# Queries and keys as three bf16 parts through a DRAM scratch into three buffers, bf16 masks and row maxima, and a new order of all engines

## The chip, the cores and the metric

The kernel runs on one core of one Trainium2 chip. The metric is the device time of one execution in microseconds, lower is better. A core has TensorE (PE in the profile; its weight loads are PEld), VectorE (DVE), ScalarE (ACT), GpSimd (POOL) and SyncE (SP), which run their own queues in order and meet at semaphores.

## The reference, cut to what matters

Two transformer layers over x of shape (16, 256, 128), 16 heads of width 8, each layer attention and then a mixture of experts, with a layer norm behind each of the four parts:

```python
x = layernorm(x + attn0(x))      # causal, no biases
x = layernorm(x + moe0(x))       # 8 experts, top 2, hidden 256, relu
x = layernorm(x + attn1(x))      # not causal, biases
x = layernorm(x + moe1(x))       # 15 experts, top 3, gelu gate, and a shared expert
# attention, for each batch b and head h (T = 256, 8 columns per head):
s = q @ k.T / sqrt(8)            # causal in layer 0
p = softmax(s); o = p @ v
```

All inputs and outputs are fp32.

## The kernel before

The work is cut into steps; a step is one batch, or one batch and one head, or one page of an expert. The 32 attention steps a = 0 to 31 are the 16 batches of layer 0 and then of layer 1. A planner (`plan` and `lay_out`) gives every step a cost, a due time from the table `PRM` and its predecessors, simulates the five engines, and so writes the one order in which every engine issues its steps. The order is fixed when the kernel is built; on the chip every engine runs its own part of it strictly in order, held back by semaphores alone.

For a batch, TensorE makes q and k with one projection (`qk`, bank M). Every fp32 matmul of the program stands in the trace as two (128 records of L1056 for 64 matmuls), and q and k are not multiplied in fp32: they are split into a rounded high part (`qk_hi`, ScalarE, type fp32r) and the rest (`qk_lo`, VectorE, fp32r), both in the tile `parts`. SyncE then stacks them with DMAs (`stack(a, u)`, half u = 8 heads) from `parts` straight into one of four buffers `QK`, 24 rows per head: hi with hi, hi with lo, lo with hi. One fp32r matmul over the stacked rows then gives nearly fp32 scores. Each head's scores are computed twice: `scores` with queries on partitions, from which VectorE takes row maxima (`row_max`), and `scores_T` with keys on partitions, which ScalarE exponentiates. Between them, the negated maxima are split in two fp32r parts (`max_neg`), transposed (`max_T`), copied (`max_keep`) and put by a DMA from ScalarE's queue (`max_rows`) into rows 96 and 97 of the same `QK` buffer, against rows of ones, so that `scores_T` comes out with the maximum already subtracted. In layer 0 a first matmul writes the causal mask (identity times a mask, both fp32r in `rmat`) into the diagonal blocks of each bank. A `QK` buffer of half a batch is refilled when `scores_T` of the half two batches earlier is done.

`weigh_V` multiplies the exponentials by V (fp32), `O_T`, `O_back` and `proj` finish the attention, and `x_T2`, `logits`, `ranks` route the tokens. When 8 (layer 1: 10, then 6) batches are routed, VectorE builds the group's table, GpSimd scatters the rows of X to expert order in DRAM with indirect DMAs (`scatter`, L877), and the pages of 256 tokens go through their expert (`page_T`, `fc1`, `fc2`). GpSimd gathers the results back (`gather`, L891), VectorE combines them, and the next layer's batch can start. GpSimd also computes the inverse standard deviations of all norms, in the same queue. There are 23, 23, 44 and 32 pages in the four groups.

```python
def free(k):                                  # PE waits here for a bank
def stack(a, u):                              # SP: parts -> QK[2a+u mod 4], three DMAs
    sp.wait_ge(st_ps.sem, st_ps.at(a - 2, 8 * u + 8))
```

Of the kernel before, what the change touches and what calls it, by code (L numbers as in the profile page):

```python
# [6 lines left out]
F32R = mybir.dt.float32r  # L7
# [21 lines left out]
PAGE = 256  # L29

# [120 lines left out]
def shared_y_bank(b):  # L151
# [17 lines left out]
       "shift": (-30.67, 4.18, -7.9, 46.33, 16.49, 43.17, -9.93, -50.66, -60.0, 2.38, -45.61, -29.2, 39.76, 32.2, -40.19, 42.55, -0.37, -36.42, 17.74, 2.5, -8.66, -6.21, 7.29, 60.0, -16.96, -0.13, -5.19, 52.25, -27.76, -60.0, -17.49, -25.48),  # L169
       "ld": (131.0, 350.8, 247.85, 156.55, 400.0), "clear": (312.1, 268.62), "comb": 330.3}  # L170


def plan():
# [18 lines left out]
    def attention(a, t):  # L192
# [3 lines left out]
        S = (0.35, 0.245)[L]  # L196
# [7 lines left out]
        add(t + qk[0], "PE", 0.87, 0.25, "qk", a, after=x + [("stack", a - 1, 0), ("stack", a - 1, 1)], bank="M")  # L204
        add(t + qk[1], "ACT", (0.64, 0.95)[L], 0.1, "qk_hi", a, after=[("qk", a)])
        add(t + qk[2], "DVE", (0.72, 0.9)[L], 0.1, "qk_lo", a, after=[("qk_hi", a)], frees="M")
        add(t + PRM["v"][ph], "PE", 0.44, 0.25, "v", a, after=x + [("weigh_V", a - 3, 3)], bank="M")
        add(t + PRM["v"][ph] + 0.6, "ACT", 0.4, 0.1, "v_keep", a, after=[("v", a)], frees="M")
        t += PRM["first"][ph]
        for u in range(2):  # L210
            heads = range(8 * u, 8 * u + 8)
            add(t, "SP", 2.03, PRM["l_stack"] if a else 7.0, "stack", a, u, after=[("qk_lo", a)] + [("scores_T", a - 2, h) for h in heads])
            t += PRM["lag_s"][ph]
            for h in heads:
                add(t, "PE", S, 0.25, "scores", a, h, after=[("stack", a, u), ("max_neg", a - 2, u)], bank=("S0", "S1")[h % 2])
# [3 lines left out]
            add(t + mx[0], "DVE", (0.68, 0.6)[L], 0.1, "max_neg", a, u, after=[("row_max", a, h) for h in heads] + [("max_T", a - 1, u)])  # L219
# [42 lines left out]
    def chunk(c, t, step):  # L262
# [70 lines left out]
    for i in range(len(X_PIECES)):  # L333
        add(PRM["ld"][0] + PRM["ld"][1] * i, "SP", 0.95 if i == 0 else 0.5, 6.0, "load_x", i, after=[("stack", max(1, 2 * i), 1)])
    add(PRM["ld"][2], "SP", 3.3, 3.0, "load_later", after=[("stack", 3, 0)])
    add(PRM["ld"][3], "DVE", 3.0, 0.1, "prepare", after=[("load_later",), ("stack", 4, 1)])
    add(PRM["ld"][3] + 60, "PE", 0.3, 0.25, "bias_rows", after=[("prepare",), ("stack", 6, 1)], bank="N")
    add(PRM["ld"][3] + 60, "DVE", 0.4, 0.1, "bias_add", after=[("bias_rows",)], frees="N")
    for k, (lo, hi) in enumerate(TAB_PIECES):
        add(PRM["ld"][4] * 0.25 + P[0] * k, "SP", 1.2 * (hi - lo), 6.0, "build_w1", k, after=[("prepare",), ("stack", 5 + k, 1)])  # L340
    for k in range(len(FILL_STEPS)):
        add(PRM["clear"][0] + PRM["clear"][1] * k, "SP", 0.5, 3.5, "clear_xs", k, after=[("stack", 1 + k // 2, k % 2)])
# [99 lines left out]
def build(nc, x_in, xT_in, cols_in, rows_in, bmat_in, rmat_in, wqk_in, wvo_in, w0_in, w1_in, w2_in, b2_in, sw1_in, out):  # L442
    ctx = ExitStack()
    with ctx:
# [13 lines left out]
        parts = sb("parts", [D, 2, 2, T], F32R)  # L458
        QK = [sb(f"QK{i}", [D, NH // 2, 2, T], F32R) for i in range(4)]
# [1156 lines left out]
```

## Time and profile before

| | |
|---|---|
| median of 3 runs | 1208.55 us (1205.19 to 1209.41) |
| span of the profiled execution, first to last instruction | 1058.9 us |
| outside the span (median less span) | 149.65 us |
| busy in the span | PE 906.3, PEld 763.1, DVE 679.9, ACT 549.4, POOL 444.0 us |
| mean granted TensorE clock | 0.927 |

The profile does not give the profiled execution a time of its own beyond its span, so what lies around the span is taken as the median less the span. Busy time of PE counts modelled ends of pipelined matmuls, so a stretch in which PE is "busy" throughout is one in which it never ran dry, not one at its peak.

### The profile page before, as it was taken

To read this page: it belongs to the slowest core of one execution; us is meant where nothing else is said; L and a number is where in the kernel's file an instruction comes from. 1 tells how busy PE (TensorE), PEld (TensorE's weight loads), DVE (VectorE), ACT (ScalarE), POOL (GpSimd) and SP (SyncE) were. 2 spreads that over 40 slices of the span, in tenths; PEclk is the share of its full clock that TensorE was granted. 3 is DMA by queue.
4 is the path that set the end of the run, shared out by engine and by line. 5 is a ranking of instruction groups with operands and counts; after the bars stand their busy time and mean duration, and the time that the engine had idled before them with its cause. 6 is when DMAs were issued, how large, how long until landed. Compare 5 with 4: busy or idle time off the path is not lost.

```text
span 1058.9 us, 23206 instructions
## 1 busy us (share of the span) xinstructions
PE 906.3 (86%) x7486; PEld 763.1 (72%) x7486; DVE 679.9 (64%) x2209; ACT 549.4 (52%) x1320; POOL 444.0 (42%) x688
## 2 busy tenths in 40 slices
PE   5899988995999996998999896899898999789910
PEld 4788878884899985766888665676666789688810
DVE  3467755673644475987655566888875565378863
ACT  1356654562655564666766474567556655334300
POOL 7000100054500075477200375325776157377774
PEclk9699998997999998999999897999989999989965
DMA  4557564555468433364667333323444789888421
GB/s 78 103 107 193 114 142 101 135 135 133 106 178 204 125 68 59 53 125 85 144 182 191 66 57 58 51 35 56 87 90 130 216 264 326 280 247 270 122 64 53
DMA packets 111752, 138.49 MB, mean 131 GB/s; under 512 B 12275, under 2 KB 86033, under 8 KB 111633
## 3 DMA queue, kind: packets, MB, share of 16 engines
q1 hardware_dynamic: 100241, 114.97, 45.9%
q0 software_dynamic: 10240, 20.99, 7.9%
q10 hardware_dynamic: 1152, 1.05, 0.6%
q8 instruction: 62, 1.02, 0.4%
q14 instruction: 57, 0.47, 0.2%
HBM read 70.25 MB, written 42.48 MB: 106 GB/s over the span
## 4 chain that ended last, share of the span: by engine, by line
PE 49%; DMA 20%; issue 8%; POOL 7%; DVE 7%; SPq 6%; ACT 2%; POOLq 0%; ACTq 0%; DVEq 0%
DMA QK<-parts 10%; PE bank_O L1132 5%; PE bank_N L1224 5%; DMA G<-yd,ypos 5%; PE bank_FH L1212 4%; POOL xs L877 4%; PE bank_S L1087 4%; PE bank_T L1110 3%; PE bank_S L1083 3%; PE bank_S L1085 3%; PE bank_T L1114 3%; SPq L736 2%; PE bank_T L1112 2%; PE bank_M L1056 2%; DMA QK<-mrow 2%
## 5 line engine op out<-in xcount | busy, mean ns | idle before, releaser
L1298 DVE TENSOR_REDUCE mp<-bank_S 128x3 f32<-128x384 f32 (+1 forms) x512 | 304.2, 620 | 133.9 <-PE bank_S L1087 91.7
L948 ACT ACTIVATE P<-bank_T 128x384 f32<-128x384 f32 (+1 forms) x512 | 260.9, 543 | 90.0 <-PE bank_T L1114 58.2
L891 POOL DMA_INDIRECT G<-yd,ypos x160 | 155.2, 970 | 76.1 <-issue 47.3
L877 POOL DMA_INDIRECT xs<-X,ypos x160 | 155.9, 974 | 48.7 <-issue 43.6
L1132 PE MATMUL bank_O<-P,V 128*32 128x256 f32 (+1 forms) x2048 | 128.8, 371 | 1.4 <-ACT P L948 1.0
L1083 PE MATMUL bank_S<-QK 96*128 96x256 f32 x512 | 112.4, 322 | 18.5 <-DMA QK<-parts 8.9
L1110 PE MATMUL bank_T<-QK 128*128 128x256 f32 x512 | 110.8, 322 | 10.6 <-ACT P L948 6.1
L828 POOL TENSOR_TENSOR rstd<-mv,half 128x2 f32<-128x2 f32 x48 | 9.6, 200 | 261.4 <-DVE mv L1351 261.1
L1085 PE MATMUL bank_S<-rmat 128*128 128x256 f32 x256 | 91.7, 358 | 22.3 <-DMA QK<-parts 21.6
L1083 PEld LDWEIGHTS bank_S<-QK 96*128 96x128 f32 x512 | 79.5, 201 | 35.8 <-DVE mp L1298 20.5
L1087 PE MATMUL bank_S<-QK 96*128 96x128 f32 (+1 forms) x512 | 104.7, 292 | 0.0
L1110 PEld LDWEIGHTS bank_T<-QK 128*128 128x128 f32 x512 | 78.7, 201 | 30.5 <-ACT P L948 20.6
L1112 PE MATMUL bank_T<-rmat 128*128 128x256 f32 x256 | 87.3, 341 | 2.4 <-DMA QK<-mrow 2.4
L1114 PE MATMUL bank_T<-QK 128*128 128x256 f32 (+1 forms) x512 | 88.7, 255 | 0.0
L955 ACT ACTIVATE OT<-bank_O 128x256 f32<-128x256 f32 x128 | 48.8, 382 | 74.1 <-PE bank_O L1132 72.8
L1132 PEld LDWEIGHTS bank_O<-P,V 128*32 128x32 f32 x2048 | 55.1, 112 | 43.1 <-issue 9.6
L1087 PEld LDWEIGHTS bank_S<-QK 96*128 96x128 f32 x512 | 85.6, 204 | 0.4
L1517 DVE SCALAR_TENSOR_TENSOR X<-G,wk,X 128x128 f32<-128x128 f32 x160 | 55.5, 351 | 45.7 <-DMA G<-yd,ypos 41.5
L1114 PEld LDWEIGHTS bank_T<-QK 128*128 128x128 f32 x512 | 81.0, 194 | 0.3
L1085 PEld LDWEIGHTS bank_S<-rmat 128*128 128x128 f32 x256 | 51.6, 202 | 33.2 <-issue 25.1
L842 POOL TENSOR_TENSOR dm<-lg,m 128x16 f32<-128x16 f32 (+1 forms) x32 | 7.5, 234 | 123.2 <-DVE m L1382 122.8
L1000 ACT ACTIVATE hT<-bank_FH,W 128x256 f32<-128x256 f32 x92 | 38.6, 470 | 39.6 <-PE bank_FH L1212 38.9
(171 smaller groups left out, 1753.3 us busy)
## 6 DMA issues: line engine op xcount, KB each, us to landing
QK<-parts SPq DMA_DIRECT2D x192, 128.0 KB
QK<-wtab SPq DMA_DIRECT2D x76, 257.0 KB, 3.9
W<-w_in SPq DMA_DIRECT2D x46, 321.0 KB, 4.0
QK<-xs SPq DMA_DIRECT2D x38, 256.0 KB, 4.3
yd<-P SPq DMA_DIRECT2D x38, 256.0 KB, 3.9
xs<-zeros SPq DMA_DIRECT2D x17, 512.0 KB, 8.1
xp<-xs SPq DMA_DIRECT2D x22, 256.0 KB, 4.1
yd<-yb SPq DMA_DIRECT2D x22, 256.0 KB, 4.0
```

The lines of the kernel that those rows point to most:

```text
L877: pool.indirect_dma_start(xs[g % 2], bass.IndirectOffsetOnAxis(ypos[L][:, 2 * b + blk, k:k + 1], 0), X[:, 2 * b + blk, :], None).then_inc( ...
L891: pool.indirect_dma_start(G[i][:, blk, k, :], None, yd[g], bass.IndirectOffsetOnAxis(ypos[L][:, 2 * b + blk, k:k + 1], 0))\
L948: act.activation(P[:, (h // 4) % 2, h % 4, 0:n], bank[("T0", "T1")[h % 2]][:, 0:n], ACT.Exp, scale=SCALE)\
L1083: m = pe.matmul(S[:, qb * T:(qb + 1) * T], Q[:, qb * D:(qb + 1) * D], K)
L1085: pe.matmul(diagonal(S), identr, mask_q, start=True, stop=False, skip_group_check=True)
L1087: m = pe.matmul(S[:, o:o + n], Q[:, qb * D:(qb + 1) * D], K[:, 0:n], start=False, stop=(qb == 1), skip_group_check=True)
L1110: m = pe.matmul(S[:, kb * T:(kb + 1) * T], K[:, kb * D:(kb + 1) * D], Q)
L1112: pe.matmul(diagonal(S), identr, mask_k, start=True, stop=False, skip_group_check=True)
L1114: m = pe.matmul(S[:, o:o + n], K[:, kb * D:(kb + 1) * D], Q[:, kb * D:T], start=False, stop=(kb == 1), skip_group_check=True)
L1132: m = pe.matmul(o, w, x, start=(kb == 0), stop=(kb == 1), skip_group_check=True)
L1298: dve.tensor_reduce(mp[:, a % 2, 0:n, h], bank[("S0", "S1")[h % 2]][:, 0:n * w] .rearrange("p (a c) -> p a c", a=n), AX.X, ALU.max).then_i ...
L1517: dve.scalar_tensor_tensor(out=t, in0=G[i][:, blk, k, :], scalar=wk[L][:, b, blk, k:k + 1], in1=t, op0=ALU.mult, op1=ALU.add).then_inc(sig ...
```

## The change

Queries and keys are split in three bf16 parts, hi, mid and low. ScalarE makes hi (`qk_hi`), VectorE the fp32 rest (`qk_rest`), ScalarE mid (`qk_mid`, new) and VectorE low (`qk_low`, new). SyncE writes the six slots to a DRAM scratch (`spread_parts`, new, two scratches by turns), and from there fills 48 rows of one whole batch buffer (`stack(a)`): hi·hi, hi·mid, mid·hi and further pairs. There are three buffers of a whole batch instead of four of half a batch; a buffer is refilled after `scores_T` of the batch three earlier. The row maxima come out of the reduction already negated and are split in three bf16 pieces by reading the upper halves of fp32 words; their transpose is a bf16 matmul and they take three rows. The mask matmul is bf16 and the fp32r table `rmat` is gone. The planner's costs and its table of due times are new, so the order of every engine changes.

```diff
-        parts = sb("parts", [D, 2, 2, T], F32R)
-        QK = [sb(f"QK{i}", [D, NH // 2, 2, T], F32R) for i in range(4)]
+        parts = sb("parts", [D, 2, 3, T], BF16)
+        rest = sb("rest", [D, 2, T])
+        QK = [sb(f"QK{i}", [D, 2, NH, T], BF16) for i in range(3)]
...
-            def stack(a, u):
-                c = 2 * a + u
+            def spread_parts(a):
                 sp.wait_ge(lo_done.sem, lo_done.all(a))
-                if a < 2:
-                    sp.wait_ge(cleared.sem, 1 + 3 * c)
-                    if c == 0:
+                if a >= 2:
+                    sp.wait_ge(stacked[(a - 2) % 3].sem, stacked[0].all((a - 2) // 3))
+                sp.dma_start(stk[a % 2].rearrange("i p t -> p i t"), slots(parts[:, :, :, :])).then_inc(spread[a % 2].sem, DMA)
+
+            def stack(a):
+                sp.wait_ge(spread[a % 2].sem, spread[a % 2].all(a // 2))
+                if a < 3:
+                    sp.wait_ge(cleared.sem, 1 + 3 * a)
+                    if a == 0:
                         sp.wait_ge(cleared_dve.sem, 2)
                 else:
-                    sp.wait_ge(st_ps.sem, st_ps.at(a - 2, 8 * u + 8))
-                p = parts[64 * u:64 * u + 64, :, :, :].bitcast(F32).rearrange("p s i t -> p (s i) t")
-                for i, pair in enumerate((p[:, 0::2, :], p[:, 0::3, :], p[:, 1:3, :])):
-                    sp.dma_start(QK[c % 4][HD * i:HD * i + HD, :, :, :].bitcast(F32), pair).then_inc(stacked[c % 4].sem, DMA)
+                    sp.wait_ge(st_ps.sem, st_ps.all(a - 3))
+                for row, n in ((0, 3), (3, 2), (5, 1)):
+                    pair = stk[a % 2].rearrange("i (d h) t -> (i d) (h t)", h=NH).rearrange("(s r) c -> r s c", s=2) if n == 3 else \
...
+                    sp.dma_start(QK[a % 3][row * HD:(row + n) * HD, :, :, :].rearrange("r s h t -> r s (h t)"), pair)\
+                        .then_inc(stacked[a % 3].sem, DMA)
...
+            def qk_mid(a):
+                act.wait_ge(rest_done.sem, rest_done.all(a))
+                act.activation(slots(parts[:, :, :, :])[:, 1::3, :], rest[:, :, :], ACT.Copy).then_inc(mid_done.sem, 1)
...
-                if h % 8 == 0:
-                    pe.wait_ge(stacked[c % 4].sem, stacked[c % 4].all(c // 4))
+                if h == 0:
+                    pe.wait_ge(stacked[a % 3].sem, stacked[a % 3].all(a // 3))
...
-                    pe.matmul(diagonal(S), identr, mask_q, start=True, stop=False, skip_group_check=True)
+                    pe.matmul(diagonal(S), identb, mask_q, start=True, stop=False, skip_group_check=True)
...
+            def qk_low(a):
+                dve.wait_ge(mid_done.sem, mid_done.all(a))
+                p = slots(parts[:, :, :, :])
+                dve.tensor_tensor(p[:, 2:4, :], rest[:, :, :], p[:, 1::3, :], ALU.subtract).then_inc(lo_done.sem, 1)
...
-       "period": (49.67, 34.69, 165.68), "first": (30.17, 13.12, 29.81, 163.03),
+       "period": (50.52, 67.62, 161.84), "first": (0.0, 36.41, 64.77, 143.39), "lag_s": (51.57, 41.8, 6.21, 26.18),
```

Two places show what the new table does. The first is TensorE at the seam of the layers: the rows just ahead of the first head of layer 1, batch 16 (`bank_S0<-QK`, L1083 before and L1099 after). `bank_T` rows are heads of `scores_T`, here of batch 15, `bank_O` is `weigh_V`. Before:

```order
L1112 MATMUL bank_T1<-rmat 128x2x128
L1114 MATMUL bank_T1<-QK2 128x256
L1114 MATMUL bank_T1<-QK2 128x128
L1140 MATMUL bank_N<-cols,OT 128x128 x4
L1096 MATMUL bank_M<-cols,neg 16x128 x2
L1112 MATMUL bank_T0<-rmat 128x2x128
L1114 MATMUL bank_T0<-QK2 128x256
L1114 MATMUL bank_T0<-QK2 128x128
L1112 MATMUL bank_T1<-rmat 128x2x128
L1114 MATMUL bank_T1<-QK2 128x256
L1114 MATMUL bank_T1<-QK2 128x128
L1083 MATMUL bank_S0<-QK0 128x256 x2
```

And with the change:

```order
L1154 MATMUL bank_N<-cols,OT 128x128 x4
L1201 MATMUL bank_N<-mk0,bmat 128x8
L1202 MATMUL bank_N<-mk0,bmat 128x8
L1203 MATMUL bank_N<-mk0,bmat 128x8
L1204 MATMUL bank_N<-mk0,bmat 128x8
L1205 MATMUL bank_N<-mk0,bmat 128x8
L1060 MATMUL bank_M<-cols,X 128x128 x2
L1154 MATMUL bank_N<-cols,OT 128x128 x4
L1085 MATMUL bank_M<-wvo,xT 128x128 x2
L1162 MATMUL bank_N<-cols,On 128x128 x2
L1099 MATMUL bank_S0<-QK1 128x256 x2
```

Before, most heads of `scores_T` of batch 15 still stood behind the first head of batch 16; now batch 15 is finished up to its output transposes (`O_T`, L1154) when batch 16 begins.

The second place is SyncE's queue in layer 0, around the refill for batch 6 (`xs` is the DRAM buffer being cleared, `wtab` a table of weights being built, `xT` the transposed input of a batch to come). Before:

```order
L715 DMA xs1<-zeros 512x1x256
L720 DMA wtab<-w1_in 256x258
L722 DMA wtab<-xG1 128x2x128
L723 DMA wtab<-b2 256x1x128
L715 DMA xs1<-zeros 512x1x256
L692 DMA xT<-xT_in 128x256
L736 DMA QK0<-parts 8x16x256 x2
L736 DMA QK0<-parts 8x8x512
L736 DMA QK1<-parts 8x16x256 x2
L736 DMA QK1<-parts 8x8x512
```

And with the change:

```order
L731 DMA wtab<-w1_in 256x258
L733 DMA wtab<-xG1 128x2x128
L734 DMA wtab<-b2 256x1x128
L726 DMA xs1<-zeros 512x1x256
L703 DMA xT<-xT_in 128x256
L726 DMA xs1<-zeros 512x1x256
L754 DMA QK0<-stk0 24x2x4096
L754 DMA QK0<-stk0 16x2x4096
L754 DMA QK0<-stk0 8x2x4096
L740 DMA stk1<-parts 128x6x256
```

The same neighbours stand ahead of the refill, which is now three DMAs for the whole batch instead of six, with the parts of the next batch sent to the scratch right behind it.

## Rows read from the trace of the kernel before

**Rows 1.** Stretches: length, busy (instructions) of PE, PEld, DVE, ACT, POOL, clock, DMA.

```profile
60.00:140.00 80.00, 78.97 (x798) 69.51 (x797) 57.84 (x194) 48.60 (x119) 7.53 (x28) 1.00 0.65 140
18.00:219.50 201.50, 188.16 (x1757) 165.57 (x1756) 131.91 (x419) 103.06 (x252) 17.97 (x57) 0.93 0.58 122
219.50:290.00 70.50, 55.72 (x547) 48.98 (x546) 41.41 (x153) 33.18 (x82) 38.70 (x59) 0.90 0.55 132
290.00:370.00 80.00, 80.00 (x675) 73.31 (x674) 35.14 (x108) 45.25 (x119) 2.51 (x10) 1.00 0.68 167
370.00:406.00 36.00, 34.88 (x362) 30.18 (x361) 27.94 (x108) 24.89 (x64) 27.36 (x46) 1.00 0.45 75
406.00:450.00 44.00, 34.75 (x293) 27.52 (x293) 33.68 (x108) 22.02 (x55) 19.94 (x37) 0.88 0.31 49
450.00:512.00 62.00, 55.00 (x473) 42.02 (x472) 48.81 (x162) 41.57 (x93) 43.99 (x69) 0.94 0.53 108
512.00:592.00 80.00, 78.04 (x616) 68.47 (x615) 41.89 (x108) 50.37 (x126) 5.06 (x14) 1.00 0.69 166
592.00:643.00 51.00, 38.61 (x337) 27.34 (x337) 30.02 (x114) 28.14 (x65) 30.27 (x49) 0.85 0.34 59
643.00:722.00 79.00, 70.36 (x564) 55.02 (x562) 66.17 (x219) 48.52 (x115) 29.44 (x66) 0.90 0.31 45
722.00:829.00 107.00, 96.35 (x831) 69.98 (x830) 75.21 (x251) 69.27 (x157) 72.89 (x106) 0.95 0.47 106
829.00:1058.90 229.90, 168.84 (x1040) 150.61 (x1039) 143.45 (x464) 79.74 (x192) 139.08 (x155) 0.88 0.67 203
```

**Rows 2.** Waits of PE from 18 to 290 us: total, times, longest.

```profile
PE bank_S L1085 <- DMA QK<-parts: 21.4, 7, 12.4
```

**Rows 3.** PE in order of time: start, length, engine, line (layer 0).

```profile
101.00 0.38 PE L1112 MATMUL bank_T<-rmat 128*128 128x256 f32 x1
...
101.81 0.38 PE L1148 MATMUL bank_N<-cols,On 128*128 128x128 f32 x2
```

**Rows 4.** Groups of 60 to 140 us: times | busy us, mean ns | idle.

```profile
L1085 PE MATMUL bank_S<-rmat 128*128 128x256 f32 x64 | 22.0, 344 | 0.7 <-DMA QK<-parts 0.7
```

**Rows 5.** The chain that ended last, 190 to 205 us: start, us, one head.

```profile
202.80 0.12 PE bank_S L1085
202.92 0.23 PE bank_S L1087 x2
```

**Rows 6.** PE in order of time: bf16 matmuls and their loads.

```profile
662.08 0.17 PE L1188 MATMUL bank_N<-mk,bmat 128*128 128x15 bf16 x1
...
662.16 0.17 PE L1191 MATMUL bank_N<-mk,bmat 128*128 128x15 bf16 x1
```

**Rows 7.** Groups of the whole span: the splits and layer 1's row maxima.

```profile
L1298 DVE TENSOR_REDUCE mp<-bank_S 128x2 f32<-128x512 f32 x256 | 167.5, 686 | 36.6 <-PE bank_S L1083 35.5
...
L1285 DVE TENSOR_TENSOR parts<-bank_M,parts 128x512 fp32r<-128x512 f32 x16 | 11.0, 686 | 5.6 <-ACT parts L912 5.6
L912 ACT ACTIVATE parts<-bank_M 128x512 fp32r<-128x512 f32 x16 | 9.5, 596 | 14.8 <-PE bank_M L1056 14.8
```

**Rows 8.** The chain that ended last, whole span: start, us, what.

```profile
138.92 6.15 SPq L696
...
150.82 10.57 DMA QK<-parts
...
195.86 6.22 DMA QK<-parts
```

**Rows 9.** DMA issues of the whole span: count, KB each, median us to landing.

```profile
QK<-wtab SPq DMA_DIRECT2D x76, 257.0 KB, 3.9
```

**Rows 10.** GpSimd's scatters of 450 to 512 us: ns min/median/max, first and last start.

```profile
L877 POOL DMA_INDIRECT xs<-X,ypos x32: 954/959/1082, 457.2 to 503.6; - x32
```

**Rows 11.** The same of 722 to 829 us.

```profile
L877 POOL DMA_INDIRECT xs<-X,ypos x60: 954/958/1103, 729.6 to 816.0; - x60
```

**Rows 12.** GpSimd's gathers of 829 us to the end, the same columns.

```profile
L891 POOL DMA_INDIRECT G<-yd,ypos x96: 940/944/1029, 918.9 to 1044.2; - x96
```

More of the change, by code:

```diff
@@ L203, in attention @@
         x = [("load_xT", a), ("load_consts",)] if L == 0 else [("x_T_keep", a), ("load_later",)]
-        add(t + qk[0], "PE", 0.87, 0.25, "qk", a, after=x + [("stack", a - 1, 0), ("stack", a - 1, 1)], bank="M")
+        add(t + qk[0], "PE", 0.87, 0.25, "qk", a, after=x + [("spread_parts", a - 1)], bank="M")
         add(t + qk[1], "ACT", (0.64, 0.95)[L], 0.1, "qk_hi", a, after=[("qk", a)])
-        add(t + qk[2], "DVE", (0.72, 0.9)[L], 0.1, "qk_lo", a, after=[("qk_hi", a)], frees="M")
+        add(t + qk[2], "DVE", (0.72, 0.9)[L], 0.1, "qk_rest", a, after=[("qk_hi", a), ("qk_low", a - 1)], frees="M")
+        add(t + qk[2], "ACT", 0.63, 0.1, "qk_mid", a, after=[("qk_rest", a)])
+        add(t + qk[2], "DVE", 0.63, 0.1, "qk_low", a, after=[("qk_mid", a)])
+        add(t + qk[2], "SP", 0.68, 3.4, "spread_parts", a, after=[("qk_low", a), ("stack", a - 2)])
         add(t + PRM["v"][ph], "PE", 0.44, 0.25, "v", a, after=x + [("weigh_V", a - 3, 3)], bank="M")
@@ L209, in attention @@
         t += PRM["first"][ph]
+        add(t, "SP", 2.03, 4.6, "stack", a, after=[("spread_parts", a), ("scores_T", a - 3, 15)])
         for u in range(2):
             heads = range(8 * u, 8 * u + 8)
-            add(t, "SP", 2.03, PRM["l_stack"] if a else 7.0, "stack", a, u, after=[("qk_lo", a)] + [("scores_T", a - 2, h) for h in heads])
             t += PRM["lag_s"][ph]
             for h in heads:
-                add(t, "PE", S, 0.25, "scores", a, h, after=[("stack", a, u), ("max_neg", a - 2, u)], bank=("S0", "S1")[h % 2])
+                add(t, "PE", S, 0.25, "scores", a, h, after=[("stack", a), ("max_T", a - 2, u)], bank=("S0", "S1")[h % 2])
                 add(t + 0.4, "DVE", (0.58, 0.71)[L], 0.1, "row_max", a, h, after=[("scores", a, h)],
@@ L218, in attention @@
                 t += PRM["step_s"][ph]
-            add(t + mx[0], "DVE", (0.68, 0.6)[L], 0.1, "max_neg", a, u, after=[("row_max", a, h) for h in heads] + [("max_T", a - 1, u)])
+            add(t + mx[0], "DVE", (0.68, 0.6)[L], 0.1, "max_neg", a, u, after=[("row_max", a, h) for h in heads])
             add(t + mx[1], "PE", 0.25, 0.25, "max_T", a, u, after=[("max_neg", a, u), ("max_rows", a - 1, u)], bank="M")
@@ L439, in all, with build @@
         return (i + 1) * self.per
[L442 removed]
+def build(nc, x_in, xT_in, cols_in, rows_in, bmat_in, wqk_in, wvo_in, w0_in, w1_in, w2_in, b2_in, sw1_in, out):
     ctx = ExitStack()
@@ L542, in build @@
         wtab = dram("wtab", (E1, D, WCOLS[1]))
+        stk = [dram(f"stk{i}", (SLOTS, D, T), BF16) for i in range(2)]
         bank = {n: ctx.enter_context(nc.psum_tensor(f"bank_{n}", [D, 2 * T], F32)) for n in BANKS}
@@ L580, in build @@
         v_kept = signal("v_kept")
-        stacked = [signal(f"stacked{i}", 3 * DMA) for i in range(4)]
+        spread = [signal(f"spread{i}", DMA) for i in range(2)]
+        stacked = [signal(f"stacked{i}", 3 * DMA) for i in range(3)]
         s_ps = signal("s_ps", NH)
@@ L588, in build @@
         m_kept = signal("m_kept", 2)
-        m_stacked = [signal(f"m_stacked{i}", DMA) for i in range(4)]
+        m_stacked = [[signal(f"m_stacked{i}{u}", DMA) for u in range(2)] for i in range(3)]
         st_ps = signal("st_ps", NH)
@@ L1057, in qk @@
                 m.then_inc(qk_ps.sem, 1)
-                held["M"] = lo_done.sem, lo_done.all(a)
+                held["M"] = rest_done.sem, rest_done.all(a)
             def v(a):
@@ L1590 @@
     mask_q = np.where(after, f32(NEG), f32(0))
-    bmat = np.concatenate([after.astype(f32), np.ones((D, D), f32)], axis=1).astype(ml_dtypes.bfloat16)
-    rmat = np.stack([np.eye(D, dtype=f32), mask_q, mask_q.transpose(1, 0)], axis=1)
+    bmat = np.concatenate([after.astype(f32), np.ones((D, D), f32), np.eye(D, dtype=f32), mask_q, mask_q.transpose(1, 0)],
+                          axis=1).astype(ml_dtypes.bfloat16)
     arrays = {
```

155 lines of the change are left out of this document (75 added, 80 removed), and 14 rows, old and new, of the table PRM.

## The prediction

> **What bounds the kernel now.** I read the profile by stretches first, cut where one thing hands over to the next: 18 us is the first head of `scores`, 219.5 the routing of batch 7 (`ranks`), 290 and 370 the first and last page of group 0, 406 the first head of layer 1, 450 the routing of batch 15, 512 and 592 the pages of group 1, 643 the first head of batch 24, 722 the routing of batch 25, 829 the first page of layer 1 [rows 1]. In layer 0's attention TensorE is never dry: 79.0 of the 80 us from 60 to 140 are busy at full clock, while VectorE has 57.8 and ScalarE 48.6 [rows 1]. 64 heads of `scores` stand in that stretch, four batches, so 20.0 us a batch [rows 4]. The waits come second: from 18 to 290 us PE waited 21.4 us for refills of `QK` (7 times, longest 12.4 us) and for hardly anything else [rows 2]. The chain says why: `x_in`'s issue held SyncE 6.2 us before a refill that took 10.6 us itself, and even an undisturbed one, at 195.9 us, takes 6.2 us [rows 8].
>
> Two further bounds are not TensorE's. Between a group's routing and its first page GpSimd must scatter: 32 scatters from 457.2 to 503.6 us sit between 450 and 512 [rows 1, 10], 60 from 729.6 to 816.0 between 722 and 829 [rows 1, 11]. And the end is GpSimd's as well: 96 gathers, one each 1.32 us, from 918.9 to 1044.2 us [rows 12]. In layer 1's attention no engine is full: 70.4 of 79 us PE, 66.2 DVE [rows 1], 0.686 us per head for the row maximum alone [rows 7].
>
> **A head in bf16.** A `scores` and a `scores_T` head of layer 0 together take 101.81 - 101.00 = 0.81 us, 0.405 each [rows 3]; in the chain's best case one takes 0.12 + 0.23 = 0.35 [rows 5]. That is three weight loads and 256 + 128 + 256 columns. In bf16 the columns stay. 256 of them took 0.12 us with the fp32r load beside them, so 640 take at most 0.30 us [rows 5]. Loads: four starts from L1188 to L1191, each with a full bf16 load ahead of it, are 0.08 us apart, 27 ns each [rows 6], so a bf16 load hides under any of the three matmuls. I take 0.29 us (bounds: 0.27, which is 640 columns at one per cycle of the 2.4 GHz level that the rows grant, and 0.35, the best fp32r head). It saves 0.115 us a head, 32 heads a batch: 3.7 us of 20.0.
>
> The Trainium skill speaks against this. "TensorE: Matmul & The Clock Gate", section "LDWEIGHTS (loading the stationary operand)", gives a load of P columns P/1.2 ns whatever the type, 107 ns for 128; an estimate from it is 3 x 107 = 320 ns a head, and the head saving would shrink by a quarter or more. Its section "Weight-path perf modes" lets non-fp32 loads of 128 columns go faster. By the first the trace disagrees (27 ns for load and matmul together), by the second it agrees.
>
> The shorter transposes of the maxima are worth about 0.1 us each, 0.2 a batch. In layer 1 a head has two matmuls of 256 columns at 0.12 us or so; at 0.107 to 0.12 the gain is 0 to 0.4 us a batch, and VectorE's 0.686 us paces those heads anyway. I count none.
>
> So TensorE needs 16.2 us per batch of layer 0. VectorE has 57.84 / 4 = 14.5 now, and `qk_low` comes to it: between nothing and 0.686, the price of the same shape from PSUM [rows 7]; I take 0.6, which makes 15.1. ScalarE has 48.6 / 4 = 12.2 and gets `qk_mid`, 0.6 [rows 7]. `max_neg` keeps its number of operations. Three engines at 16.2, 15.1 and 12.8 don't mesh perfectly: I take 17.3 us a batch.
>
> **Refills.** Before, each half batch took three DMAs and its landing 6.2 to 10.6 us [rows 8]. Now `parts` goes to DRAM and back. The trip out has no row; I take 2 to 8 us around it, and it stands beside work: `qk` of a batch now stands 23 to 28 us of TensorE work ahead of its first head in batches 3 to 10, where it was 9 to 11. What can be late is `stack(a)`, which waits for the last `scores_T` of batch a-3. Counted in the new order with the durations above, TensorE has 9.1, 5.2, 6.0, 6.7, 6.9, 7.9, 9.8, 9.0, 12.8, 11.9, 10.2, 17.8, 6.9 us of work between that and the first head, for a = 3 to 15, and 4.8 to 8.5 for five batches of layer 1 (19 and 22 to 25); elsewhere over 11. The landing of 768 KB in three DMAs is bounded by 3.9 us, that of 257 KB in long runs [rows 9], and 10.6 [rows 8]; its runs are 8 KB against 1 KB, so I take 7, and a shortfall of under 2 us for five batches, 5 us in all. Behind `stack(a)` on SyncE wait the next `spread_parts`, `xT`, the clearing of `xs` and `wtab`'s pieces, all due later than the head. The longest stalls (12.4 us) came with SyncE held by loads ahead of a refill needed at once; `qk` early and whole batches ahead remove that, in part.
>
> **The new order.** All steps keep their predecessors; what changes is which stand together. Stretch by stretch, before and after:
> - start to first head: 18, after 21 (`spread_parts` 2 to 4 us, two more splits 1.2, against two fewer fp32r tables).
> - to batch 7 routed: 201.5. Ten batches less 2.7 us each, less 8 of the stalls of this stretch, plus 11 more heads of `scores` now placed here (3) and 5 for late refills: 173.
> - to the first page: 70.5. TensorE now has about 44 us of work here, so GpSimd's scatters set it. Group 1 shows their price, 62 us from routing to page [rows 1, 10]: 62.
> - pages of group 0: 80; PE full, 8 more heads: 79.
> - to batch 16's first head: 36. `scores` of batch 15 moved forward, so only `scores_T` of 14 and 15 and their tail are left, 27 us of work, against a chain: page store, gather, combine, norm, projection, four splits, scratch, stack. Before, batch 16's first head came 36 us after the last page with TensorE nearly full; I take 37, the scratch eating what the shorter queue gives.
> - to batch 15 routed: 44. Batch 15 is through `O_T` when batch 16 starts, where its heads still stood behind; what is left is `proj`, norm, `logits`, `ranks`: 14. This is the largest single term.
> - to group 1's first page: 62, again GpSimd's: 62 [rows 10].
> - its pages: 80; 4 us more work: 84.
> - to batch 24: 51, with 38.6 us busy. One batch more stands in cover (32 us of work): 47.
> - to batch 25 routed: 79; 24 heads and 7 `weigh_V` more stand here: 90.
> - to layer 1's first page: 107; 60 scatters, 86 us, with table, landing and load around 98 to 107 [rows 11]: 104.
> - to the end: 229.9, same pages, 96 gathers in the same queue [rows 12]: 230.
>
> Sum: 21+173+62+79+37+14+62+84+47+90+104+230 = 1003 us of span. The profiled execution has 1058.9; what lies around it, 149.65 us by the median of the runs, I leave: 1003 + 150 = **1153 us**, 4.6% faster.
>
> **The rivals.**
> - VectorE becomes the bound. From 643 to 722 us it was 84% busy, and that may be as full as it gets. Then a batch of layer 0 needs 15.1 / 0.84 = 18.0 and one of layer 1 0.7 more: 11 x 0.7 + 16 x 0.7 = 19 us. Time 1172.
> - bf16 loads cost what fp32r ones do, so a head stays at 0.35 to 0.405. Then 28 us of the second and third stretch are not there, the rest stands: 1180. Against it stand the 27 ns of rows 6. The page's rule above gives a third of that loss.
> - Slower: the refill is late in every batch. A landing of L us costs L less the work listed above. At 10 us that is 23 us in layer 0 and 13 in layer 1, giving 1183; at 8, 13 us; the change is eaten from about L = 11.5 on, and at 13 the time is some 1230. For it: 768 KB go to 48 partitions, and clearing DMAs of 512 KB stand right ahead in SyncE's queue, as when a refill took 10.6 us. Against it: eight times longer runs, and 257 KB in 3.9 us.
> - The largest term fails: after the seam the wait for batch 16 moves into the routing of 15 or to the group's pages. 20 us back: 1173.
>
> **How the numbers follow.** Forecast case 0.55 (its own range 1130 to 1175), VectorE 0.15, loads 0.05, late refills without loss of the whole gain 0.08, seam 0.09, slower 0.08. Between them 1125 to 1192 holds eight in ten. Less than 0.5% (6 us) is about what a measurement of this kernel can't tell from no change. Faster 0.88, same 0.04, slower 0.08.
>
> **What would show it.** After: starts of heads 0.29 us apart in layer 0 (right) or 0.35 (wrong); 17 to 17.5 us a batch from 60 to 140 us, PE still fullest; waits for `QK<-stk` under 10 us in sum; first page near 256 us, page 23 near 448, first page of layer 1 near 773, 34, 64 and 56 us earlier; scatters adjoining both. Wrong would be: a refill from issue to landing over 9 us, long waits of PE ahead of a page (scatter dearer than 1.3 us), or a part outside the span that grew.

## The result and the profile after

The changed kernel takes 1245.14 us (median of 4 runs, 1242.41 to 1255.65) against 1208.36 us for the kernel before beside it: a ratio of 1.030, 95% interval [1.024, 1.036]. It is slower, by 37 us; 1153 was forecast, and a range of 1125 to 1192.

First a correction to what the numbers are made against. The profiled execution of this result has a span of 1253.9 us and is itself the run of 1255.65 us, so 1.75 us lie outside a span, not 149.65. The kernel before takes 1055 to 1057 us on three chips (called the quicker chips below) and 1208 us on a fourth, as in this result. On which chip the profile of before that the forecast worked from was taken isn't known, but its span of 1058.9 us fits the quicker ones. On one of those the changed kernel takes 1086 us, at almost the same ratio (1.028). All ratios below are within one chip; differences in us between two of the quicker chips can be off by some 2 us. The rows of the change that follow are those of its repetition on a quicker chip, span 1085.7 us, which answer to the rows of before.

The stretches of the change, cut at the same events as [rows 1] (columns as there):

```profile
23.00:243.00 220.00, 182.62 (x1839) 137.37 (x1840) 142.30 (x445) 108.81 (x269) 15.78 (x55) 0.89 0.64 141
243.00:303.70 60.70, 52.09 (x565) 40.14 (x563) 42.88 (x159) 35.25 (x87) 38.96 (x59) 0.94 0.61 139
303.70:389.60 85.90, 81.88 (x708) 71.19 (x709) 39.83 (x128) 47.77 (x124) 3.75 (x14) 0.96 0.60 159
389.60:437.30 47.70, 36.03 (x361) 24.94 (x360) 22.39 (x108) 28.61 (x74) 31.93 (x53) 0.83 0.31 64
437.30:449.80 12.50, 9.22 (x53) 5.35 (x52) 11.19 (x33) 5.22 (x14) 9.17 (x17) 0.77 0.84 146
449.80:499.80 50.00, 43.93 (x345) 23.16 (x343) 43.65 (x119) 27.35 (x59) 36.50 (x50) 0.81 0.53 121
499.80:604.10 104.30, 89.13 (x680) 72.11 (x681) 53.92 (x159) 61.80 (x152) 16.14 (x37) 0.93 0.61 148
604.10:656.60 52.50, 40.68 (x367) 25.64 (x366) 37.96 (x130) 30.96 (x73) 29.96 (x50) 0.87 0.44 80
656.60:752.40 95.80, 80.39 (x754) 51.40 (x755) 77.34 (x255) 66.00 (x155) 31.29 (x71) 0.93 0.34 60
752.40:855.50 103.10, 84.91 (x755) 48.78 (x756) 69.56 (x234) 64.82 (x144) 73.96 (x105) 0.92 0.43 100
855.50:1085.70 230.20, 169.53 (x1064) 150.10 (x1063) 144.51 (x472) 82.14 (x196) 140.57 (x157) 0.89 0.69 210
```

Beside the stretches of before and of the forecast (us; "bare" is a later experiment in which TensorE waits neither for `xT` nor, behind the first head, for refills):

| stretch | before | forecast | change | bare |
|---|---|---|---|---|
| to the first head | 17.8 | 21 | 23.0 | 22.1 |
| to batch 7 routed | 201.7 | 173 | 220.0 | 173.4 |
| to the first page | 70.0 | 62 | 60.7 | 55.1 |
| pages of group 0 | 78.9 | 79 | 85.9 | 78.9 |
| to batch 16's first head | 37.4 | 37 | 47.7 | 41.4 |
| to batch 15 routed | 43.9 | 14 | 12.5 | 12.8 |
| to group 1's first page | 62.0 | 62 | 50.0 | 50.2 |
| its pages | 80.2 | 84 | 104.3 | 86.7 |
| to batch 24's first head | 51.2 | 47 | 52.5 | 42.3 |
| to batch 25 routed | 79.2 | 90 | 95.8 | 80.8 |
| to layer 1's first page | 103.6 | 104 | 103.1 | 99.1 |
| to the end | 233.0 | 230 | 230.2 | 229.6 |

The change's span is 83 us over the forecast's 1003, and the second stretch alone gives 47 of them. What TensorE waited for, of the change, 18 to 290 us, then the whole span (total us, times, longest), against one kind of wait in [rows 2]:

```profile
PE bank_S L1101 <- DMA QK<-stk: 24.2, 6, 8.1
PE bank_M L1073 <- DMA xT<-xT_in: 22.8, 7, 4.7
```

```profile
PE bank_S L1099 <- DMA QK<-stk: 29.8, 9, 5.3
PE bank_S L1101 <- DMA QK<-stk: 27.7, 7, 8.1
PE bank_M L1073 <- DMA xT<-xT_in: 22.8, 7, 4.7
```

The profile of the timed result, on the slower chip, has the same two from 18 to 290 us:

```profile
PE bank_S L1101 <- DMA QK<-stk: 25.7, 6, 8.3
PE bank_M L1073 <- DMA xT<-xT_in: 22.8, 6, 6.0
```

Of the 24.2 us of the rows before these, 8.1 are the first head's own, at 23.0 us, ahead of the stretch. Inside it, from 23 to 243 us, TensorE waited 16.1 us for refills (five times) and 15.3 us for `xT` (five times). Its busy time there is 182.6 us, where the bare kernel does the same work in 166.9, at 0.97 of the clock and not 0.89. 16.1 + 15.3 + 15.8 = 47.2 us is the stretch's miss (47.0; the bare kernel's stretch is 46.6 us shorter): waits, and the clock that was lost with them. For the clock's part, the trace has TensorE busy at the 1.2 GHz level for 40.1 us of this stretch in the change and for 9.6 us of it in the bare kernel. Taking work at that level to go half as fast as at 2.4 GHz, half of the difference, 15.3 us (an estimate), is what the level cost. The two kinds of wait have a place each in the chain of the change (start, us, what; L754 issues a refill, L707 loads `X`, L726 clears `xs`):

```profile
101.83 0.33 SPq L754
102.20 0.35 SPq L754
102.61 9.42 DMA QK<-stk
112.17 0.27 PE bank_S L1101
...
129.49 7.75 SPq L707
137.28 2.54 SPq L726
139.86 0.66 SPq L726
140.63 5.18 DMA xT<-xT_in
145.94 1.10 PE bank_M L1073 x4
...
148.65 9.91 DMA QK<-stk
158.70 0.37 PE bank_S L1101
```

The refill of 768 KB takes 9.4 us behind its last issue, where [rows 8] had 6.2 for half a batch, 384 KB, and 10.3 us from the first issue to the first head. `xT`, which was worth 6.6 us of wait in the whole kernel before, is late behind SyncE's queue. For batches 3 to 10 the first issue of `stack(a)` lies within 0.1 us of the end of `scores_T` of batch a-3, and for batches 4 to 10 the first head follows 10.1 to 10.8 us behind it: with three buffers the refill can't start earlier than that.

### The profile page after: what moved, and what is told of

It reads as the page before. It is cut to its first block, busy times and chain, and to the rows that moved or that the text cites. A ratio compares the mean times of both kernels' runs of the same rounds, so it can differ in the third digit from the quotient of the medians.

```text
span 1253.9 us, 23136 instructions
## 1 busy us (share of the span) xinstructions
PE 926.2 (74%) x7486; PEld 681.2 (54%) x7486; DVE 697.1 (56%) x2241; ACT 565.4 (45%) x1351; POOL 442.2 (35%) x685
## 4 chain that ended last, share of the span: by engine, by line
PE 47%; DMA 16%; another core or an unknown queue 11%; DVE 9%; issue 7%; SPq 6%; ACT 2%; POOL 1%; ACTq 0%; DVEq 0%; POOLq 0%
DMA QK<-stk 10%; PE bank_O L1146 6%; PE bank_FH L1226 4%; PE bank_T L1124 4%; PE bank_N L1238 4%; PE bank_S L1099 4%; DVE mp L1319 3%; SPq L726 3%; PE bank_M L1073 2%; DMA xT<-xT_in 2%; PE bank_S L1103 2%; PE bank_T L1128 2%; PE bank_S L1101 2%; DMA stk<-parts 2%
## 5 line engine op out<-in xcount | busy, mean ns | idle before, releaser
L1099 PE MATMUL bank_S<-QK 96*128 96x256 bf16 x512 | 107.0, 314 | 67.6 <-DVE mp L1319 32.4
L847 POOL TENSOR_TENSOR rstd<-mv,half 128x2 f32<-128x2 f32 x48 | 11.2, 234 | 356.6 <-DVE mv L1368 356.2
L1124 PE MATMUL bank_T<-QK 128*128 128x256 bf16 x512 | 101.4, 305 | 22.3 <-issue 11.6
L1099 PEld LDWEIGHTS bank_S<-QK 96*128 96x128 bf16 x512 | 47.2, 108 | 104.0 <-DVE mp L1319 52.1
L1101 PE MATMUL bank_S<-bmat 128*128 128x256 bf16 x256 | 74.9, 293 | 34.4 <-DMA QK<-stk 30.2
L1103 PE MATMUL bank_S<-QK 96*128 96x128 bf16 (+1 forms) x512 | 87.9, 261 | 0.0
L1128 PE MATMUL bank_T<-QK 128*128 128x256 bf16 (+1 forms) x512 | 86.6, 261 | 0.0
L1126 PE MATMUL bank_T<-bmat 128*128 128x256 bf16 x256 | 75.0, 293 | 14.0 <-issue 10.9
L1124 PEld LDWEIGHTS bank_T<-QK 128*128 128x128 bf16 x512 | 47.3, 107 | 55.8 <-ACT P L967 23.0
L1073 PE MATMUL bank_M<-xT,wqk 128*128 128x256 f32 x128 | 47.0, 504 | 28.4 <-DMA xT<-xT_in 22.8
L1103 PEld LDWEIGHTS bank_S<-QK 96*128 96x128 bf16 x512 | 53.4, 104 | 7.6 <-issue 0.6
L1128 PEld LDWEIGHTS bank_T<-QK 128*128 128x128 bf16 x512 | 53.3, 104 | 7.2 <-issue 0.3
L1101 PEld LDWEIGHTS bank_S<-bmat 128*128 128x128 bf16 x256 | 26.2, 102 | 49.5 <-issue 36.4
```

The lines of the kernel that those rows point to most:

```text
L1073: m = pe.matmul(M[:, side * T:(side + 1) * T], wqk[:, L, side * D:(side + 1) * D], xT[:, a % 2, :])
L1099: m = pe.matmul(S[:, qb * T:(qb + 1) * T], Q[:, qb * D:(qb + 1) * D], K)
L1101: pe.matmul(diagonal(S), identb, mask_q, start=True, stop=False, skip_group_check=True)
L1103: m = pe.matmul(S[:, o:o + n], Q[:, qb * D:(qb + 1) * D], K[:, 0:n], start=False, stop=(qb == 1), skip_group_check=True)
L1124: m = pe.matmul(S[:, kb * T:(kb + 1) * T], K[:, kb * D:(kb + 1) * D], Q)
L1126: pe.matmul(diagonal(S), identb, mask_k, start=True, stop=False, skip_group_check=True)
```

## The experiments

Ratios are to the kernel before on the same chip. The first eleven kernels ran on the quicker chips (the first three, the next four and the four behind them on one each), the last three on the slower one.

**Which part: code or table.** The kernel before again, the changed code under the old table of due times, the old code under the new table, and the change again. The edit of the second, which the third makes the other way round in the kernel before (the whole of `PRM`):

```diff
-       "period": (50.52, 67.62, 161.84), "first": (0.0, 36.41, 64.77, 143.39), "lag_s": (51.57, 41.8, 6.21, 26.18),
...
+       "period": (49.67, 34.69, 165.68), "first": (30.17, 13.12, 29.81, 163.03),
...
```

> The kernel before, unchanged, profiled again. Profile theory: the profiled execution that the prediction was read from (span 1058.9 us) is not like the timed runs (1208 us); a second profile will have a span within 5 us of its time, near 1206 us, with longer waits for refills than the 21.4 us read from 18 to 290 us. Rival: some 150 us always lie outside the span of this kernel, and the span is near 1059 us again.

> The changed kernel with the table of due times (PRM) of the kernel before; the planner makes its order from it with the new steps and costs. Order theory (the new table is what costs): the time falls to 1210 us or below. Refill theory (the batch refill of 768 KB through DRAM lands in 10 us and is needed in less): the refill is the same and the old table knows nothing of it, so it stays at 1240 us or above.

> The kernel before with the new table of due times. Order theory: slower than 1208 us by as much as the change was, some 1245 us. Refill theory: the table alone moves it by less than half of that, 1190 to 1225 us.

> The changed kernel unchanged, so that its trace and its ratio stand beside the variants on one chip. The chip of the first three runs gave 1055 us to the kernel before, that of the result 1208. If only the chip's speed differs, the ratio is 1.03 again. If the change is more sensitive than the kernel before to what differs, it is another: the new table on the old kernel cost 3.8% and the new code under the old table 6.6%, so anything from 1.03 to 1.10 would fit.

1055.9 us (1.0005 [0.997, 1.004]); 1123.1 (1.066 [1.059, 1.072]); 1095.0 (1.038 [1.032, 1.044]); 1085.8 (1.028 [1.025, 1.032]). The kernel before has a span of 1053.6 us in a run of 1055.42, so neither expectation for it came: the span is the short one again, and nothing of 150 us lies outside. The next two were expected in us of the slower chip, so only their ratios answer: the new code under the old table is on the refill theory's side (1.026 and more), the old code under the new table on the order theory's (some 1.03). Either part alone is slower than both together: code and table belong together, and with the waits in place neither is the hidden gain. The old table in the changed kernel reached batch 7's routing after 189.6 us instead of 220, and lost it on the pages of group 1 (115.0 us, 104.3 in the change) and at the end (276.5, 230.2 in the change).

**Where a refill lands, and who clears `xs`.** One kernel puts the last 24 of the 48 rows on partitions 64 to 87 instead of 24 to 47 (the same bytes and DMAs, the same sum over rows); one has GpSimd issue the clearing of `xs` at the same places of the plan; one has both.

```diff
-                    sp.dma_start(QK[a % 3][row * HD:(row + n) * HD, :, :, :].rearrange("r s h t -> r s (h t)"), pair)\
+                    at = row * HD if n == 3 else row * HD + 40
+                    sp.dma_start(QK[a % 3][at:at + n * HD, :, :, :].rearrange("r s h t -> r s (h t)"), pair)\
```

```diff
-                sp.dma_start(dst, zeros[:, :].unsqueeze(1).broadcast_to((D, hi - lo, T))).then_inc(xs_clear[i if lo < PAGES[i] else i + 2].sem, DMA)
+                pool.dma_start(dst, zeros[:, :].unsqueeze(1).broadcast_to((D, hi - lo, T))).then_inc(xs_clear[i if lo < PAGES[i] else i + 2].sem, DMA)
```

> The changed kernel with rows 24 to 47 of the refill put on partitions 64 to 87 instead (they are multiplied just the same, all else is zero there). Landing theory: a refill takes 10 us because 48 neighbouring partitions take 768 KB, as 24 took half of it in 5 before; spread wider it lands in 5 to 7 us, packets of 8192 B fall from 873 ns to under 600, and the time falls by 25 us or more. Rival (the order and SyncE's queue set it, the landing is what the long packets cost anyway): packets stay over 800 ns, time within 10 us of the changed kernel.

> The changed kernel with the 21 clearing DMAs of xs issued by GpSimd, at the same places of the plan. SyncE theory: two clears in a row hold SyncE's queue 8 to 9 us in each of batches 5 to 11, the load of xT waits behind, then qk; without them PE's waits for xT (22.8 us) go and the time falls by 20 us or more. Landing theory: xT is no longer waited for but refills are, time falls by less than 10 us.

> Both edits together. If landing and SyncE's queue are the two costs of the change in layer 0, this is faster than either by 30 us and more against the changed kernel; if the order alone is to blame, it stays within 15 us of it.

Split rows: 1056.7 us, 1.001 [0.999, 1.004], 29 us less than the change. Clears alone: 1091.2, 1.033 [1.027, 1.038], nothing. Both: 1052.5, 0.998 [0.994, 1.001]. So the clears that stood "right ahead in SyncE's queue" were not what the refills cost, and the place of half their rows was worth 29 us. A single refill got only a little shorter by it, far from the 5 to 7 us that were expected. In the chain of the kernel with split rows, two refills of layer 0 (start, us; 8.97 and 9.42 in the change's chain at the same two batches):

```profile
75.37 8.48 DMA QK<-stk
...
97.47 7.96 DMA QK<-stk
```

Waits for refills fell from 57.5 to 35.9 us. That undoes the loss, but brings none of the forecast's 56 us, and `xT` stays late (PE's waits, whole span):

```profile
PE bank_M L1074 <- DMA xT<-xT_in: 26.0, 8, 4.8
PE bank_S L1102 <- DMA QK<-stk: 18.9, 7, 6.4
PE bank_S L1100 <- DMA QK<-stk: 17.0, 8, 4.6
```

**Without the waits.** Refills that move one row per DMA from the third (before) or fourth (change) batch on leave out the rest of the rows, but keep every issue, semaphore and order. `xT` gets eight buffers and an earlier place in SyncE's queue; nothing else in any queue moves.

```diff
-                    sp.dma_start(QK[a % 3][row * HD:(row + n) * HD, :, :, :].rearrange("r s h t -> r s (h t)"), pair)\
+                    cut = slice(0, HD * n if a < 3 else 1)
+                    sp.dma_start(QK[a % 3][row * HD:(row + n) * HD, :, :, :].rearrange("r s h t -> r s (h t)")[cut], pair[cut])\
```

```diff
-        xT = sb("xT", [D, 2, T])
+        xT = sb("xT", [D, 8, T])
...
+                if a >= 8:
+                    sp.wait_ge(v_ps.sem, v_ps.all(a - 8))
+                    sp.wait_ge(qk_ps.sem, qk_ps.all(a - 8))
...
+for a in range(3, NB):
+    here, there = PLAN.index(("load_xT", (a,))), PLAN.index(("stack", (a - 2,)))
+    if here > there:
+        PLAN.insert(there, PLAN.pop(here))
```

> The kernel before, but from batch 2 on each of the three DMAs of a refill moves one row of eight (the other rows keep older values; this part of the computation is left out). It had 26 us of waits for refills. Theory A (what the change saves on TensorE is real and is eaten by waits for its inputs): the removal frees at most those 26 us here, 0.975 to 0.99 of before. Theory B (the new order and its own chains cost what bf16 saves): the same for this kernel; it is the other half of the pair with the next run.

> The changed kernel, each refill DMA from batch 3 on moving one row only (the rest is left out). Theory A: the 57 us of waits for QK<-stk go; waits for xT (23 us) stay, so about 1030 to 1040 us, 0.98 of before, some 50 us under the changed kernel. Theory B: the order waits for something else instead and the time stays above 1050 us, no better than with half the rows on other partitions.

> Half the rows of a refill on partitions 64 to 87 as before, plus eight buffers of xT, each load put ahead of stack(a - 2) in SyncE's queue instead of behind a later stack. Theory A: 26 us of waits of TensorE for xT, and the half-clock stretches behind them, go; at least half comes back as time: 1030 to 1043 us, 0.98 to 0.99 of before, routing of batch 7 near 215 us instead of 235. Theory B: qk comes early but nothing that ends a stretch waits for it; under 5 us, 1052 us or more.

> The changed kernel with one-row refills and early xT loads together: what is left when TensorE waits neither for refills nor for xT. Theory A: the forecast's own time, batches of 17.3 us in layer 0, routing of batch 7 near 200 us, and 1000 to 1020 us on this chip, 0.95 to 0.965 of before. Theory B: batches stay near 20 us because VectorE, ScalarE or the order itself paces them, and the time stays at or above 1040 us.

| kernel | us | ratio |
|---|---|---|
| before, one-row refills | 1011.6 | 0.958 [0.954, 0.962] |
| change, one-row refills | 1006.8 | 0.951 [0.946, 0.956] |
| change, split rows, early `xT` | 1028.8 | 0.974 [0.969, 0.978] |
| change, one-row refills, early `xT` ("bare") | 975.9 | 0.924 [0.920, 0.928] |

Theory A holds. The bare kernel's batches of layer 0 are 16.6 us apart (first heads of batches 3 and 10 at 68.2 and 184.6 us), those of before with one-row refills 19.4 (75.8 and 211.9 us): the 2.7 us a batch of the forecast are there. Its stretch of 60 to 140 us, and below it that of before with one-row refills:

```profile
60.00:140.00 80.00, 79.62 (x932) 63.56 (x932) 68.09 (x225) 55.28 (x141) 8.79 (x32) 1.00 0.50 156
```

```profile
60.00:140.00 80.00, 79.72 (x810) 70.69 (x809) 59.02 (x197) 49.35 (x120) 7.53 (x28) 1.00 0.36 109
```

TensorE is full in both, and starts 79 heads of `scores` against 64 in the same time. VectorE at 68.1 of 80 doesn't hold it back. Each miss was on the good side: the expectations had at most 26 us of gain for the kernel before, 1030 us or more for the change with one-row refills and 1000 or more for the bare kernel. TensorE's waits for the change's refills were 57.5 us, 49.4 without the first head's, and one-row refills gave 79.0; those of before were 26.2 us, and gave 45.2. The rest can be the clock, as above, the chains that a late batch had pushed back, and the bytes that are no longer moved (129.3 MB in the bare kernel, 150.7 in the change); no run splits it. The kernel with four buffers below moves all bytes, and its second stretch is as short as the bare one's (172.1 us, 173.4).

The kernel with split rows and early `xT` is 2.7% faster than before and computes the whole reference. It has no wait for `xT` in 18 to 290 us; what is left there (5.9 of it the first head's) is

```profile
PE bank_S L1106 <- DMA QK<-stk: 17.1, 6, 5.9
```

**Start or landing.** Three kernels on the slower chip, where before has 1208.4 us. They ask whether it is the late start of a refill or its slow landing that costs. A fourth `QK` buffer (`stack(a)` then waits for `scores_T` of a-4 and stands right behind `spread_parts(a)` in SyncE's queue; four `xT` buffers), with split rows and without, and three buffers with split rows, early `xT` and GpSimd's clears.

```diff
-        QK = [sb(f"QK{i}", [D, 2, NH, T], BF16) for i in range(3)]
+        QK = [sb(f"QK{i}", [D, 2, NH, T], BF16) for i in range(4)]
-                    sp.wait_ge(st_ps.sem, st_ps.all(a - 3))
+                    sp.wait_ge(st_ps.sem, st_ps.all(a - 4))
+for a in range(3, NA):
+    there, here = PLAN.index(("spread_parts", (a,))) + 1, PLAN.index(("stack", (a,)))
+    PLAN.insert(there, PLAN.pop(here))
```

> Ports and early xT (four buffers of xT) as in the last run of that name, plus a fourth whole batch QK buffer: stack(a) waits for scores_T of batch a-4 and stands right behind spread_parts(a) in SyncE's queue. Theory C (the 51 us between that run and its one-row twin are refills that start late, at the very end of scores_T of a-3): the waits for QK<-stk fall from 36 us to near nothing and the time to 985 to 1000 us. Theory D (they are contention and landing of 10 us itself, wherever it starts): above 1015 us.

> The same with all 48 rows on partitions 0 to 47 again. Theory C: a refill that starts early enough may take 10 us; within 5 us of the run with split rows, so the partitions stop to matter. Theory D: the slow landing still costs what it cost with three buffers, 20 us or more above the run with split rows.

> Three buffers, split rows, early xT, and the clearing of xs issued by GpSimd. The clears gave 4 us beside split rows alone; with the queue freed of xT they should give no more: 1024 to 1029 us. If SyncE's queue was still late for refills, 1015 us or less.

1163.4 us, 0.961 [0.953, 0.970]; 1186.9, 0.984 [0.976, 0.992]; 1190.1, 0.985 [0.979, 0.991]. The times expected were for a quicker chip, so only the differences answer. With the fourth buffer and split rows the second stretch is 172.1 us, the forecast's 173, where three buffers took 187.4; the wait left in 18 to 193 us is the first refill's. Windows and waits of that kernel:

```profile
20.80:192.90 172.10, 165.90 (x1838) 127.58 (x1839) 140.10 (x444) 107.41 (x269) 16.17 (x56) 0.98 0.75 175
```

```profile
PE bank_S L1109 <- DMA QK<-stk: 5.9, 1, 5.9
```

Over the whole kernel the start is worth 26.7 us (1190.1 less 1163.4, if the clears and the number of `xT` buffers are worth nothing) and the landing 23.5 us even with four buffers (1186.9 less 1163.4), so theory C is right for the waits of layer 0, where behind the first head neither kernel waits for a refill, and wrong for the rest. C had the two within 5 us of each other, D had 20 us or more. The two profiled executions differ by 18.3 us. 5.9 of them lie in the second stretch (178.0 against 172.1; what made them isn't shown), and 10.8 where batches of layer 1 wait in a chain for their input and the refill starts only when that is ready (pages of group 1, 99.4 against 93.6 us; to batch 25's routing 95.7 against 90.7). There a slow landing costs even with four buffers. The kernel with four buffers, 3.9% faster than before and 6.6% faster than the change, is the fastest of those that compute everything.

## Why the prediction was wrong

**Right.** The head in bf16. Starts of heads in the trace of the four-buffer kernel (start, us, engine, line; two heads of `scores_T`, two of `scores`, one of `scores_T`):

```profile
100.10 0.27 PE L1134 MATMUL bank_T<-bmat 128*128 128x256 bf16 x1
...
100.37 0.27 PE L1134 MATMUL bank_T<-bmat 128*128 128x256 bf16 x1
...
100.65 0.27 PE L1109 MATMUL bank_S<-bmat 128*128 128x256 bf16 x1
...
100.92 0.27 PE L1109 MATMUL bank_S<-bmat 128*128 128x256 bf16 x1
...
101.20 0.27 PE L1134 MATMUL bank_T<-bmat 128*128 128x256 bf16 x1
```

0.275 us each; 0.29 was taken, 0.27 was the lower bound. Two rows of weight loads (PEld) from the same place, and one of an fp32r load of before:

```profile
100.65 0.21 PEld L1111 LDWEIGHTS bank_S<-QK 96*128 96x128 bf16 x2
...
100.82 0.10 PEld L1109 LDWEIGHTS bank_S<-bmat 128*128 128x128 bf16 x1
```

```profile
60.52 0.19 PEld L1085 LDWEIGHTS bank_S<-rmat 128*128 128x128 f32 x1
```

The Trainium skill ("TensorE: Matmul & The Clock Gate", section "LDWEIGHTS (loading the stationary operand)") gives 107 ns for a load of 128 columns. For one load the trace agrees: a bf16 load takes 0.10 us. The estimate of 320 ns a head, which adds three of them up, it refutes: the next load starts at 100.82, before the row of two ends at 100.86, and a head takes 0.275 us. Section "Weight-path perf modes" of that page, by which loads other than fp32 can go faster, agrees with 0.10 against 0.19 us, though no run here shows that this mode is the reason. So the prediction's reading of [rows 6], 27 ns for load and matmul together, was of the spacing of starts; a load itself is longer, and hides.

The batch of 17.3 us (16.6 in the bare kernel), the 173 us with all inputs in time (173.4 and 172.1), the 14 us to batch 15's routing (12.5), GpSimd's stretches (60.7, 50.0 and 103.1) and the end (230.2) came as worked out or better: the bare kernel's span is 972.3 us against the forecast's 1003. The splits cost `qk_low` 0.70 and `qk_mid` 0.63 us where 0.6 was taken, harmlessly.

**Wrong: "so I take 7, and a shortfall of under 2 us for five batches, 5 us in all".** In the chain of the change refills take 9.0 to 10.5 us behind their last issue, near the other bound of 10.6. The reason for choosing 7, that its runs are 8 times longer, was not enough. Per byte the landing did get quicker (768 KB in 9.4 us, 384 KB in 6.2), but the whole batch must land before its first head. And the 3.9 us of [rows 9] are of 257 KB spread over all 128 partitions, 2 KB each, where a refill puts 16 KB into each of 48. Moving rows to other partitions, with the same runs, shortened it. The prediction's own formula (landing less the TensorE work listed) at 10 us says 23 us in layer 0; 19.6 were measured there for batches 3 to 15. For layer 1 it says 13, and 29.8 were measured: the list of work ahead presumes that the refill starts when its buffer comes free, where for batches 20, 21, 24 to 27 and 31 it started 3 to 33 us later, when `spread_parts` of the batch had landed. 21.4 of the 29.8 us are waits of batches 20, 21, 26, 27 and 31, which the prediction had as covered ("elsewhere over 11"). And a us of wait cost up to 1.6 us of time (79.0 / 49.4, the bytes left out included), not one.

**Wrong: "Behind `stack(a)` on SyncE wait the next `spread_parts`, `xT`, ... all due later than the head".** This is the unpriced step. `stack(a)` holds SyncE until `scores_T` of a-3 ends (75.9 us of SyncE's idle time to 290 us, 11 times); `load_xT` issues after it and behind loads and clears, and `qk` stands in TensorE's queue in order, so every head behind it waits. Waits of 22.8 us; moved ahead, 27.8 us of time came back beside split rows (1056.7 to 1028.8) and 30.9 beside one-row refills (1006.8 to 975.9). The text listed what is queued behind the waiting instruction, and then didn't ask for each what TensorE step waits for it.

**Wrong: "what lies around it, 149.65 us by the median of the runs, I leave".** It was the difference between a profile and times of unlike executions, most likely of two chips, and not a part of a run; 1.8 us lie outside. It changed the size of the result, not its sign.

**The stretches behind the second.** 20 of the 83 us lie in the pages of group 1 (104.3 us, 84 taken); TensorE waited 11.2 us there for the refills of batches 20 to 22. The largest single term, the routing of batch 15, came (12.5 for 14 us), but batch 16's first head came 10.7 us later than taken, and 4.4 us later even in the bare kernel; no run splits that chain further. Against them, group 1's first page followed its routing in 50.0 us where 62 were taken: luck, as nothing in the working said so. The working has two slips besides: the terms listed for the second stretch (201.5 less 27, less 8, plus 3, plus 5) make 174.5 and not 173, and a scatter "dearer than 1.3 us" was no sign of being wrong, as [rows 10] have them 1.5 us apart.

**The rivals.** The slower one was the case: the refill late in every batch through 48 partitions. It had a chance of 0.08. Its working put the break-even at 11.5 us; with the late `xT` beside it, 10 us was past it already, and each us of wait cost more than one. VectorE as the bound didn't come: it was to make a batch 18.0 us, and the bare kernel has 16.6 with VectorE 85% busy (68.1 of 80). The loads in bf16 stayed hidden, and the wait for batch 16 did not move into the routing of 15. The balance on the quicker chips: what refills and `xT` cost the change, 109.9 us (change less bare); the gain of the bare kernel over the one-row kernel before, 35.7 us, of which some is `xT`, as the latter still waits 6.7 us for it; what the old refills cost the kernel before, 45.2 us. 109.9 - 35.7 - 45.2 = 29.0 is the loss on those chips, as it must be.

What stays open: how much of the gain of 35.7 us is the code's and how much the new order's, since code and table were exchanged only with their waits in place; how short a landing can get, since only one other place for the rows was tried; and why the place matters.

## What to carry to other kernels

Longer runs alone do not make a transfer of three times the bytes land in time: take its price from a row with as many bytes per partition. Here rows moved from partitions 24 to 47 to 64 to 87 landed sooner, so try other places for the rows of a contraction when a transfer has a deadline. When a ring goes from four half buffers to three whole ones, work out when its refill can start, not only how long it takes; a refill whose start is the last reader's end needs its whole landing covered by work on the waiting engine. And for an in-order DMA queue with a long-waiting instruction, follow each later entry to the engine step that needs it and its place in that engine's order, as for the head itself.

## What was not expected of the hardware

- 768 KB into 48 neighbouring partitions took 9.0 to 9.9 us in layer 0, behind the last issue, 79 to 87 GB/s; with half of them moved to partitions 64 to 87, 8.0 to 8.5 us. The refills' packets of 8192 bytes fell from a median of 854 to 701 ns. That was worth 29 us of kernel time.
- Three chips run the kernel before at 1055 to 1057 us and one at 1208. Little of the difference is in layer 0's attention: the second stretch of the change is 220.0 us on the one kind and 228.3 on the other, that of split rows with early `xT` and three buffers 186.4 and, with GpSimd's clears, 187.4. Of the 168 us between the two spans of the change, 76 lie behind the first page of layer 1, where gathers and pages are (305.9 us against 230.2). In the timed result's chain (share of the span):

```profile
PE 47%; DMA 16%; another core or an unknown queue 11%; DVE 9%; issue 7%; SPq 6%; ACT 2%; POOL 1%; ACTq 0%; DVEq 0%; POOLq 0%
```

Neither the kernel before nor the change has such a share on the quicker chips. What the unknown queue is, and whether it is the reason, no run here tells.
- With waits of up to 5 us ahead of first heads and projections, TensorE was granted the 1.2 GHz level for 47.8 of the 220 us of the change's second stretch, a mean of 0.89. The bare kernel, with the same instructions and none of these waits, had it for 10.2 of 173.4 us, a mean of 0.97.
